# Experts' stage of a fused attention and mixture-of-experts kernel: token rows transposed by DMA on SyncE's queue

## The reference

```python
qkv = x @ w_attn.T                      # 16 heads of width 16, causal linear attention in chunks of 128
y = num / (den[..., None] + 1e-06)
attention = y @ w_proj.T

gate_logits = einsum('bsd,ed->bse', x, gate_w) + gate_b + expert_bias
top_idx = argmax(gate_logits, axis=-1)  # one of 8 experts for each token
for e in range(8):
    h = relu(einsum('bsd,df->bsf', x, w1[e]) + b1[e])      # 256 -> 1024
    y = einsum('bsf,fd->bsd', h, w2[e]) + b2[e]            # 1024 -> 256
    out = out + (top_idx == e)[..., None] * y
```

## Time and profile before

| | us |
|---|---|
| median of 3 runs | 585.15 |
| the 3 runs | 585.15, 588.65, 582.88 |
| the profiled execution | 581.22 |
| its span, first to last instruction | 579.4 |
| TensorE busy in the span | 507.9 (88%) |

### The profile page before, as it was taken

One profiled execution on the slowest core, in us unless ns is written; L12 is line 12 of the kernel. 1 busy time (PEld: TensorE's weight loads), 2 busy tenths in 40 slices (PEclk: granted clock), 3 DMA queues, 4 the chain that ended last, 5 costly groups with the idle time before them and its releaser, 6 DMA issues.

```text
span 579.4 us, 19546 instructions
## 1 busy us (share of the span) xinstructions
PE 507.9 (88%) x7097; PEld 414.2 (71%) x7097; DVE 446.2 (77%) x944; ACT 300.7 (52%) x567; POOL 333.2 (58%) x447
## 2 busy tenths in 40 slices
PE   3589999999999999999987249989989989998992
PEld 1468888788777788777865148868868868887871
DVE  3779899899999989899887937767666766666772
ACT  0546878878778787777764213333323333333320
POOL 2556888888898887988844522434442433342421
PEclk9679999999999999999999659999999999999997
DMA  8322645546456455464332421221212122221000
GB/s 276 108 73 66 195 130 179 157 156 194 142 162 184 148 174 167 154 182 133 109 104 77 146 72 39 66 69 58 84 52 68 58 70 63 67 64 41 30 6 1
DMA packets 34025, 62.58 MB, mean 108 GB/s; under 512 B 5517, under 2 KB 9998, under 8 KB 33808
## 3 DMA queue, kind: packets, MB, share of 16 engines
q1 hardware_dynamic: 28944, 48.74, 27.3%
q0 software_dynamic: 4992, 12.60, 7.2%
HBM read 50.57 MB, written 13.50 MB: 111 GB/s over the span
## 4 chain that ended last, share of the span: by engine, by line
PE 45%; POOL 35%; issue 9%; DVE 6%; DMA 1%; ACT 1%; POOLq 0%; DVEq 0%
PE ps L550 18%; PE ps L564 18%; POOL AR L1104 15%; POOL W L1112 10%; POOL XR L1097 3%; POOL nr L1082 2%; PE ps L528 2%; POOL rsn L1088 2%; POOL nr L1084 1%; PE ps L341 1%; PE ps L378 1%; POOL nr L1086 1%; PE ps L407 1%; DVE XR L871 1%; PE ps L312 1%
## 5 line engine op out<-in xcount | busy, mean ns | idle before, releaser
L550 PEld LDWEIGHTS ps<-AR,W 128*128 x1872 | 131.5, 98 | 40.2 <-issue 1.2
L564 PE MATMUL ps<-W,ST 128*128 x624 | 150.8, 326 | 7.1 <-issue 7.1
L550 PE MATMUL ps<-AR,W 128*128 128x128 f16 x1872 | 155.9, 220 | 0.8 <-ACT AR L1054 0.8
L1150 POOL DMA_INDIRECT out<-AR x39 | 39.6, 1016 | 128.1 <-DVE AR L933 123.3
L1112 POOL TENSOR_TENSOR W<-ST,W 128x512 f16<-128x512 f32 x64 | 77.3, 1208 | 50.5 <-ACT W L1015 50.1
L1104 POOL TENSOR_SCALAR AR<-AR,CT 128x512 f16<-128x512 f16 x64 | 101.5, 1595 | 6.3 <-DVE AR L672 6.3
L901 DVE SCALAR_TENSOR_TENSOR ST<-ps,TAs,B1S 128x512 f32<-128x512 f32 x78 | 58.4, 749 | 59.1 <-PE ps L550 58.7
L679 DVE SCALAR_TENSOR_TENSOR AR<-ps,SV,CT 128x512 f32<-128x512 f32 x128 | 90.1, 746 | 15.6 <-PE ps L378 13.2
L1063 ACT ACTIVATE ST<-ST 128x512 f16<-128x512 f32 x78 | 49.2, 630 | 96.5 <-DVE ST L901 93.2
L913 DVE SCALAR_TENSOR_TENSOR ST<-ST 128x512 f16<-128x512 f32 x78 | 53.8, 689 | 15.6 <-ACT ST L1063 14.9
L1145 POOL DMA_INDIRECT AR<-scr,AR x39 | 47.8, 1225 | 23.4 <-issue 11.3
(11 more groups left out here) (148 smaller groups left out, 819.7 us busy)
## 6 DMA issues: line engine op xcount, KB each, us to landing
ST<-in_w SPq DMA_DIRECT2D x128, 256.0 KB, 4.4
scr<-XR SPq DMA_DIRECT2D x32, 256.0 KB, 2.1
XR<-in_x SPq DMA_DIRECT2D x32, 128.0 KB, 5.3
AR<-in_b SPq DMA_DIRECT2D x1, 1024.0 KB, 4.9
AR<-in_wall SPq DMA_DIRECT2D x1, 776.0 KB, 4.5
AR<-scr,AR POOLq DMA_INDIRECT x39, 3.6
out<-AR POOLq DMA_INDIRECT x39
AR<-in_wp SPq DMA_DIRECT2D x1, 256.0 KB, 5.9
```

The source lines that it names most:

```text
L550: a = e.matmul(dst, W[:, off:off + 57472][:, bass.ds(at[s], 128)], XT16[s % 2][:, xl * 256 + k * 128:xl * 256 + (k + 1) * 128], start=(n = ...
L564: a = e.matmul(PS[4 + s % 2][:, 0:w], src[h % 4][:, fs], W[:, off:off + 57344 + w][:, bass.ds(at[s], w)], start=(f == 0 and w == 512), sto ...
```

## The change

Four DMA transposes a slot, issued by SyncE and each of one 128x128 piece of 16-bit values, go from `XG[s % 4]` straight into `XT16[s % 2]`. They wait for the slot's gather (`d_gat`) and, from slot 2 on, for the whole first product of slot s - 2 (`t_g1` at 2s - 2). g1(s, 0) waits for all four (a new semaphore for each of the two buffers, `d_xt`, raised by 64 a slot). TensorE's and ScalarE's `tx` and the PSUM tile `PT` are gone, and gather(s) waits for `d_xt` in place of `t_tx`.

```diff
--- before.py
+++ after.py
@@ -180,7 +180,6 @@
         H32 = [ST[:, i * 512:(i + 1) * 512] for i in range(2)]
         HH = [ST[:, 2048 + i * 256:2304 + i * 256].bitcast(F16) for i in range(4)]
         HL2 = [ST[:, 3072 + i * 256:3328 + i * 256].bitcast(F16) for i in range(4)]
-        PT = PS[6][:, 0:256].bitcast(F16)
 
         scr = nc.dram_tensor("scr", [NT, 512], F32, kind="Internal").ap()
         outr = out.rearrange("b t d -> (b t) d")
@@ -228,6 +227,7 @@
         d_wm = [sem(f"d_wm{i}") for i in range(4)]
         d_ws = [sem(f"d_ws{i}") for i in range(4)]
         d_gat = [sem(f"d_gat{i}") for i in range(NG)]
+        d_xt = [sem(f"d_xt{i}") for i in range(2)]
         d_sca = [sem(f"d_sca{i}") for i in range(3)]
 
         p_ones, p_id, p_one16, p_tri, p_v32 = (sem(n) for n in ("p_ones", "p_id", "p_one16", "p_tri", "p_v32"))
@@ -247,7 +247,7 @@
         v_o16, t_cnt, v_es, v_bo, v_ao, t_ids, v_ids, p_xg0 = (
             sem(n) for n in ("v_o16", "t_cnt", "v_es", "v_bo", "v_ao", "t_ids", "v_ids", "p_xg0"))
 
-        v_rb, t_tx, a_tx, v_out, t_g2 = (sem(f"f_{n}") for n in ("rb", "ptx", "tx", "out", "g2"))
+        v_rb, v_out, t_g2 = (sem(f"f_{n}") for n in ("rb", "out", "g2"))
 
         t_g1, v_h, a_hh, v_hl, t_hd = (sem(f"f_{n}") for n in ("g1", "h", "hh", "hl", "hd"))
 
@@ -303,6 +303,14 @@
                     e.wait_ge(v_wmx, NW)
                     e.dma_start(LC, cst2).then_inc(d_cst2, 16)
             e.dma_start(B2, b2).then_inc(d_b2, 16)
+            for s in range(NS):
+                e.wait_ge(d_gat[s % NG], 16 * (s // NG + 1))
+                if s >= 2:
+                    e.wait_ge(t_g1, 2 * s - 2)
+                x16 = XG[s % NG][:, 0:256].bitcast(F16)
+                for i in range(4):
+                    e.dma_start(XT16[s % 2][:, i * 128:(i + 1) * 128], x16[:, i * 128:(i + 1) * 128],
+                                transpose=True).then_inc(d_xt[s % 2], 16)
 
         def tensor(e):
             e.wait_ge(p_ones, 1)
@@ -519,15 +527,6 @@
                 a = e.matmul(PS[1][:, 0:NS], AO[c // 8][:, c % 8, :], BO[:, c, :], start=(c == 0), stop=(c == NC - 1))
             a.then_inc(t_ids, 1)
 
-            def tx(s):
-                e.wait_ge(d_gat[s % NG], 16 * (s // NG + 1))
-                if s >= 1:
-                    e.wait_ge(a_tx, s)
-                x16 = XG[s % NG][:, 0:256].bitcast(F16)
-                for i in range(4):
-                    a = e.transpose(PT[:, i * 128:(i + 1) * 128], x16[:, i * 128:(i + 1) * 128], id16[:, :])
-                a.then_inc(t_tx, 1)
-
             at = {}
 
             def expert(s):
@@ -538,7 +537,7 @@
                 h = 2 * s + f // 4
                 dst = PS[h % 4][:, (f % 4) * 128:(f % 4 + 1) * 128]
                 if f == 0:
-                    e.wait_ge(a_tx, s + 1)
+                    e.wait_ge(d_xt[s % 2], 64 * (s // 2 + 1))
                     if s == 0:
                         e.wait_ge(p_wlo, 8 * E)
 
@@ -570,13 +569,10 @@
 
             e.wait_ge(v_es, 1)
             expert(0)
-            tx(0)
             for t in range(8 * NS + LAG):
                 s, f = t // 8, t % 8
                 if s < NS:
                     g1(s, f)
-                    if f == 2 and s + 1 < NS:
-                        tx(s + 1)
                     if f == 4 and s + 1 < NS:
                         expert(s + 1)
                 if t >= LAG:
@@ -1047,12 +1043,6 @@
                     relu(p - 1)
                     exp(p - 1)
 
-            def tx(s):
-                e.wait_ge(t_tx, s + 1)
-                if s >= 2:
-                    e.wait_ge(t_g1, 2 * (s - 2) + 2)
-                e.activation(XT16[s % 2], PT, ACT.Copy).then_inc(a_tx, 1)
-
             def high(h):
                 e.wait_ge(v_h, h + 1)
                 if h >= 4:
@@ -1062,10 +1052,7 @@
                         e.wait_ge(t_hd, h // 2 - 1)
                 e.activation(HH[h % 4], H32[h % 2], ACT.Relu).then_inc(a_hh, 1)
 
-            tx(0)
             for s in range(NS):
-                if s + 1 < NS:
-                    tx(s + 1)
                 high(2 * s)
                 high(2 * s + 1)
 
@@ -1141,7 +1128,7 @@
             def gather(s):
                 if s >= NG:
                     e.wait_ge(v_rb, s - NG + 1)
-                    e.wait_ge(t_tx, s - NG + 1)
+                    e.wait_ge(d_xt[s % 2], 64 * ((s - NG) // 2 + 1))
                 e.indirect_dma_start(XG[s % NG], None, scr, bass.IndirectOffsetOnAxis(ids[:, s:s + 1], 0),
                                      bounds_check=NT - 1, oob_is_err=False).then_inc(d_gat[s % NG], 16)
```

## The result

The changed kernel takes 621.61 us (median of 4 runs, 620.48 to 622.69) against 584.01 (median of 4, 581.82 to 588.65): ratio 1.063, 95% interval 1.056 to 1.070. Forecast were 630 us and slower. Its profiled execution took 622.59 us, with a span of 620.4.

The account below looks back on a forecast made before the run. TensorE's list was taken to bound the experts' stage. 341.0 + 0.4 + 39 x 6.7 = 602.7, plus tail 20.8, register loads 3.5 and 1.8 outside the span, made 628.8; forecast 630 us, range 576 to 700.

Parts of the forecast that it names:

- the two-buffer rule: Experts' stage: a slot's transposes wait for the first product two slots earlier, so two slots take at least g + L.
- P: Slot period in the experts' stage, max(g, (g + L)/2) and no less than 4c: 6.7 us.
- g: TensorE's work for one slot in the experts' stage, without the transposes: 5.28 us.
- L: Time from the end of G(s - 2) to TensorE's restart: 1.0 + 0.43 + 4 x 1.67 + 0.05 = 8.2 us.
- c: What one DMA transpose holds its queue, one in flight after another: 2.1 - 0.43 = 1.67 us.
- T(s): The four DMA transposes of slot s, which must land before that slot's first product can start.
- G(s - 2): First product of slot s - 2 on TensorE; its end lets T(s) start.
- the hand-over to SyncE: Part of L from TensorE's last matmul to the waiting engine: taken as 1.0 us, from ScalarE's 1.24.
- bound from below: Low end for c: transposes overlap like plain loads, costing 0.43 us of issue each, with one landing of 2.1 us.
- like plain DMAs: Rival: transposes on SyncE's queue overlap and all is hidden, L = 4.5 us, about 577 us; chance 0.14.
- The clock: Rival: TensorE's clock drops in the waits, at half clock g is 10.6 us, up to 780 us; chance 0.05.
- The gather's lead: Last gather lands at 553.1 us, T(38) wants it at 554.1: just enough with P = 5.28, more with 6.7.

Follow-up runs that it names:

- (2): The changed kernel with two of the four transposes a slot from slot 2 on: 588.17 us, ratio 1.009.
- (3): The changed kernel with three buffers for the transposed tokens: 602.89 us; with the gathers also one place earlier in GpSimd's list: 588.40 us.
- (4): The changed kernel with two more transposes a slot, into tiles that nothing reads: 693.68 us, ratio 1.193.
- (6): The changed kernel with one transpose of 128 rows by 512 columns a slot in place of four: 581.67 us, ratio to before 0.998.
- the floor: The kernel before with the tokens of slots 0 and 1 alone transposed, later slots reusing old buffer contents: 576.84 us, ratio 0.990.
- experiment 1: Same run as the floor: the kernel before without the transposes after slots 0 and 1, 576.84 us.
- experiments 2 and 3: Three variants of the changed kernel: two transposes a slot from slot 2 (588.17 us), three buffers (602.89), three buffers and earlier gathers (588.40).
- eight: The changed kernel with each transpose cut into two of 64 rows, eight a slot, same bytes: 787.18 us in one run.

## Why the prediction was right, and where it wasn't

**What bounds the stage, and the two-buffer rule.** Right. P = max(g, (g + L)/2, the queue) is what the runs follow: fewer pieces bring the slot back to TensorE's own time (2), one more buffer takes the rule away (3), six pieces put the queue in front at the P computed ahead (4), one issue in place of four hides all (6). Two things came otherwise. The prediction had the queue of transposes busy without a break, since 4c and (g + L)/2 both gave 6.7; SyncE is held for 203 of 254.9 us, and 25 of the 39 T(s) start at the end of G(s - 2), 13 behind the transposes ahead of them. And TensorE was to wait 1.4 us in nearly every slot; it waits that long in about every second one. With both buffers in step, T(s) starts at the end of G(s - 2) and G(s) has to wait for it, while T(s + 1) follows T(s) at once and lands about when G(s) ends. The rule gives the mean of such a pair.

**The terms of L.** The sum, 8.2 us, was 1 us too long, and its parts err both ways: the hand-over to SyncE by 0.8 too long, the four issues by 1.7, the way from the last issue's end to TensorE, for which 0.05 stood, by 1.5 too short. In the trace of after, where SyncE waits for TensorE it goes on 0.08 us (median; mean 0.2) after the last matmul's end, not 1.0: ScalarE's 1.24 us said nothing about SyncE's queue. Four issues take 5.37 us on average, from the first start to the last end; the last transpose lands at TensorE 1.2 to 3.0 us after that, 1.6 on average. With the 0.2 that makes 7.15, and with g = 5.4 as the floor's slots have it, (5.4 + 7.15)/2 = 6.28 for a slot with nothing special. The 36 slots then make 226 us; the measured 237.5 have four register loads more (7.6) and two clock drops (3.4).

**The step that failed in kind: c.** I took 1.67 us as one transpose in flight after another, and 0.087 us a packet from SyncE's mean as the floor of its data part. What the runs show in its place is an issue of 1.23 us on SyncE, whatever it moves (1.23 for 64x128, 1.23 for 128x128, 1.19 for 128x512), and data that cost little. The queue's packets in 343 to 600 us of the kernel after:

```profile
q1 hardware_dynamic: 24960, 5.13, 10.7%
```

0.107 x 16 x 257 / 24960 = 0.018 us each, a fifth of the mean that I took over from packets over six times as large. A fifth of these packets are of 4 bytes; those of 256 bytes take 0.020 us, so the data of a 128x128 piece, 8 packets on each engine, take 0.16 us and not 0.7. That c came near the truth (1.30 on average, with the long issues) was luck: the wrong story had a similar price. The right mechanism stood in the prediction as its bound from below, issues that follow one another and one landing at the end, but with 0.43 us for an issue and not 1.30. The rival *like plain DMAs* was right for the transfer and wrong for the issue. The Trainium skill ("Advanced Engine Details and Errata", X-Bar Transpose: as fast as regular DMAs) agrees with the packets (the 128 plain ones of 256 bytes on SyncE's queue in the kernel before take 0.018 us each, the transposing ones 0.020), and not with the issue, 1.23 against 0.33 to 0.47 us. Its price of 1309 ns for a 128x128 piece ("VectorE: DVE Perf Modes", the three transpose paths) is near the 1.28 us from one issue to the next, but 128x512 holds SyncE no longer. Had I held to it as a price of the piece, I should have forecast 603 and missed what it is a price of.

**The sum.** 630 against 621.6. P with the register loads was forecast as 244.7 us for 36 slots and measured as 237.5. That a register load would be half absorbed was wrong: the sum above comes out only with all of the 7.6 us. The gain from the removed transposes was taken as 8.5 us and is 5.2 over the 36 slots (experiment 1). The start: by the prediction's terms G(0) begins at 341.0 + 0.4 + 6.7 = 348.1, 5.7 us late; measured from the first gather's issue it was 4.9 late (9.9 against 5.0), and 7.8 at G(2), half clock in G(0) included, which no term of the prediction had. That 630 came within 8.4 us is in part luck: L and the start were taken too long, while g (5.28, measured 5.39) and the register loads were taken too short, and the first gather came 2.5 us later than in the kernel before.

**The clock.** Given a chance of 0.05 as a stage-long drop, it came as two short ones of 1.7 us each. One follows a wait of 2.43 us, the other a register load of 1.98 us. But TensorE's longest wait behind the stage's beginning, 3.53 us up to 517.04, is followed by full clock:

```profile
515.00:520.00 5.00, 2.96 (x34) 2.34 (x35) 0.76 (x2) 0.10 (x1) 1.42 (x2) 1.00 0.37 102
```

So the length of the wait alone doesn't decide, and what does stays open. As the waits grow, so do the drops: 0 in the kernel before, 2 in the changed one, 16 with six pieces, 30 with eight.

**The gather's lead.** Right that it is enough for two buffers: in the trace of after no T(s) but T(0) starts at its gather's landing. Right too that it is next: with three buffers it was worth 14.5 us.

**What stays open.** Some issues take 1.7 to 2.9 us in place of 1.23. In the profiles of the changed kernel and of the three in experiments 2 and 3, all 58 issues of over 1.7 us have an instruction fetch of the core beginning within the issue or 0.8 us ahead of it, and only 84 of the 492 short ones do; in the other seven profiles with DMA transposes it is 81 of 81 long ones and 124 of 911 short ones. Why some fetches delay an issue and others don't wasn't found, and nothing was run that moves the fetches. Issuing the transposes from two queues wasn't tried: the Trainium skill ("DMA: Bandwidth & Descriptors", silent corruption) says that two transposing streams in flight can silently corrupt each other; no run here shows it. The 0.09 us of experiment 1 has no named cause.

## What to carry to other kernels

Before you replace an engine's work by DMAs, count the issues and ask what one holds its queue for: a DMA transpose took 1.2 us of SyncE here, for 16 KB or 128 KB alike, so the widest form that the layout allows comes first (40 us here). With two buffers a batch's whole latency has to fit into one slot of the consumer, (g + L)/2 otherwise; a third buffer helps only as far as what feeds the batch has lead as well. And what four TensorE transposes in a full stream of matmuls cost was 0.14 us a slot, so there was never more than 1.0% to gain.

## What the runs showed of the hardware

- A DMA transpose from SBUF to SBUF holds the issuing sequencer for 1.23 us (64x128 and 128x128) or 1.19 us (128x512), 16-bit values; its packets of 256 bytes take 0.020 us each, plain ones of that size 0.018.
- It lands 2.2 to 4.1 us after its issue begins, median 2.3 (128x128, last of a slot), or 2.4 to 5.8, median 3.0 (128x512). Of two of 128x256 the second has a median of 3.7.
- SyncE goes on 0.08 us after a matmul ends, while ScalarE begins 1.24 us after it.
- Instruction fetches of the core and long issues of transposes coincide (139 of 139, against 208 of 1403 short ones); the cause is not shown.
- After a wait of 2.43 us and after a register load of 1.98 us TensorE's granted clock fell to 0.5 (1.2 GHz) for 3.4 us, at a price of 1.7 us. After a wait of 3.53 us it stayed at 1.00, and so it did over the four register loads of some 1.8 us in the kernel before.
